# Second attention of a two-layer macaron block: ScalarE passes of one and of two heads, four turns over three PSUM banks, D products issued twice

## The reference, cut to what matters

```
q, k, v = split_heads(x @ Wq.T), split_heads(x @ Wk.T), split_heads(x @ Wv.T)
diff_sq = maximum(|q|^2 + |k|^2 - 2 q.k, 0)
denom   = maximum((1 - |q|^2) * (1 - |k|^2), 1e-6)
cosh    = maximum(1 + 2 * diff_sq / denom, 1)
distance = arccosh(cosh)
attn = softmax(-distance)
out  = merge_heads(attn @ v) @ Wo.T
x = x + out
```

## Time and profile before

| | us |
|---|---|
| median of 3 runs | 3502.58 (3499.26 to 3506.87) |
| the profiled execution | 3507.83 |
| its span, first to last instruction | 3506.1 |
| mean granted TensorE clock over the span | 0.847 |
| busy in the span: PE, DVE, ACT, POOL | 2925.6, 2228.4, 1880.1, 872.3 |
| `relu` (line 1475), first and last start | 1841.0, 3011.5 |

### The profile page before, as it was taken

How to read it: one execution, slowest core, us unless ns; L and a number is a source line. 1 busy time by engine, 2 the same in 40 slices (tenths; PEclk the granted TensorE clock), 3 DMA queues, 4 the chain that set the end, 5 groups by cost and what they waited for, 6 DMA issues and landing times. The chain is left out here.

```text
span 3506.1 us, 52449 instructions
## 1 busy us (share of the span) xinstructions
PE 2925.6 (83%) x17862; PEld 2166.3 (62%) x17862; DVE 2228.4 (64%) x5046; ACT 1880.1 (54%) x1988; POOL 872.3 (25%) x584
## 2 busy tenths in 40 slices
PE   5999968888689996999966878678687777579999
PEld 4888846666578885999963333233333333269998
DVE  5555557777655556666657767676675676366665
ACT  2222246767422222343327888878888788633333
POOL 1000010000000001000015564664655565410000
PEclk9999979999899997999986656666766666689999
DMA  2000000000000001000000000000000000010000
GB/s 79 0 0 0 0 1 1 0 0 0 0 1 0 0 0 48 0 0 0 0 0 1 0 0 0 0 0 0 0 0 0 0 0 0 4 45 0 0 0 24
DMA packets 3188, 17.98 MB, mean 5 GB/s; under 512 B 1088, under 2 KB 2112, under 8 KB 2112
## 3 DMA queue, kind: packets, MB, share of 16 engines
q1 hardware_dynamic: 3136, 17.32, 1.3%
HBM read 15.22 MB, written 2.10 MB: 5 GB/s over the span
## 5 line engine op out<-in xcount | busy, mean ns | idle before, releaser
L1402 POOL TENSOR_TENSOR A_Y<-A_Y,A_U 128x2048 f32<-128x2048 f32 x96 | 433.6, 4548 | 402.0 <-ACT A_U L1444 402.0
L1475 DVE TENSOR_SCALAR A_U<-ps 128x1024 f32<-128x1024 f32 x256 | 309.4, 1219 | 165.2 <-PE ps L1606 83.8
L1618 PE MATMUL ps<-A_QT,A_KT 9*128 9x512 f32 x512 | 275.3, 631 | 127.6 <-DVE A_U L1483 127.2
L140 POOL TENSOR_TENSOR rstd<-var_eps,half_neg 128x4 f32<-128x4 f32 x45 | 49.8, 1106 | 1288.6 <-DVE var_eps L120 1182.4
L1483 DVE SCALAR_TENSOR_TENSOR A_U<-ps,A_U 128x1024 f32<-128x1024 f32 x256 | 311.8, 1218 | 40.4 <-PE ps L1618 40.3
L1606 PE MATMUL ps<-A_QT,A_KT 28*128 28x512 f32 x512 | 249.3, 612 | 100.8 <-DVE A_U L1475 99.4
L257 ACT ACTIVATE F1b_act<-ps 128x512 f32<-128x512 f32 x256 | 153.3, 599 | 247.3 <-PE ps L223 231.2
L257 ACT ACTIVATE F1a_act<-ps 128x512 f32<-128x512 f32 x256 | 153.3, 599 | 242.9 <-PE ps L223 226.6
L1618 PEld LDWEIGHTS ps<-A_QT,A_KT 9*128 9x128 f32 x512 | 112.3, 271 | 251.6 <-DVE A_U L1483 215.4
L1590 PE MATMUL ps<-A_Y,A_VA 128*32 128x512 f32 x768 | 246.0, 779 | 16.7 <-ACT A_Y L1451 16.7
L257 ACT ACTIVATE F0b_act<-ps 128x512 f32<-128x512 f32 x160 | 95.7, 598 | 273.3 <-PE ps L223 273.3
(11 more groups left out here) (338 smaller groups left out, 6634.1 us busy)
## 6 DMA issues: line engine op xcount, KB each, us to landing
dn<-in_down SPq DMA_DIRECT2D x2, 2048.0 KB, 12.1
stage<-in_up SPq DMA_DIRECT2D x1, 2560.0 KB, 9.4
X<-in_x SPq DMA_DIRECT2D x1, 2048.0 KB, 7.7
F1a_up<-in_up SPq DMA_DIRECT2D x1, 2048.0 KB, 8.1
F1b_up<-in_up SPq DMA_DIRECT2D x1, 2048.0 KB, 7.2
out_x<-X SPq DMA_DIRECT2D x1, 2048.0 KB, 6.3
dn<-in_down SPq DMA_DIRECT2D x1, 1280.0 KB, 12.3
qkv_w_s<-in_w_qkv SPq DMA_DIRECT2D x2, 192.0 KB
```

Of the source, the lines that this page charges most:

```text
L1402: eng.tensor_tensor(flat(y_slot(h)), flat(y_slot(h)), flat(Um[:, h % UR]), ALU.add).then_inc(s["t_ready"], 1)
L1475: eng.tensor_scalar(u_half(h, half), d_pair(n), 0.0, None, ALU.max).then_inc(s["dp_vector"], 1)
L1618: last = eng.matmul(ps[:, 4 + b, :], KT[r:r + 9, h // 2, kt * P:(kt + 1) * P], QT[r:r + 9, h // 2, :], start=True, stop=True)
```

## The change

- ScalarE: of each four heads, the first two have square-root passes of their own (2048 elements), the last two a joined one. Ln and Exp stay joined.
- GpSimd: `apply_norm_gpsimd` stands behind the adds of heads 4 to 7 and `assemble_gpsimd`; `keep_norm_gpsimd` behind all adds.
- TensorE: `difference` issues its two products twice, in the order 0, 1, 0, 1, into the same two banks with the same data. `turn_four` does the four turns in front of bursts 0 and 3 over banks 6, 4, 5 and 6, and the pair's outputs follow them in one run. q, k and v are projected into banks 6, 4 and 5 one behind the other, then come all outputs of pair 7, and then the waits for all three takes. In a burst, a pair's outputs are k tile 0 in step 5, k tile 1 in step 6, k tiles 2 and 3 in step 7.
- The back turns of the chunk before start one step earlier in burst 1, and the transposes and scores of its norm move from burst 2 to steps 4 and 5 of burst 3. VectorE's side follows, and its copies of the outputs move into step 4 of bursts 0, 2 and 3.
- New waits: banks 4 and 5 must be free of factor products (`u_ready`), bank 6 of the scores (`lg_copied`) and of the output projection (`x_added`).

The core of the diff:

```
...
-def take_v_vector(eng, k):
+def take_v_vector(eng, k, bank):
     eng.wait_ge(s["v_done"], k + 1)
     eng.wait_ge(s["pvh_done"], k * PAIRS + 1)
...
-        rows_of_bank(ROWS)).then_inc(s["v_taken"], 1)
+        rows_of_bank(bank)).then_inc(s["v_taken"], 1)
...
     eng.wait_ge(s["qk_tr"], k * TURNS + i + 1)
+WINDOW_BANKS = (6, 4, 5, 6)
...
             for h in range(0, 4):
-            if not first:
-                apply_norm_gpsimd(eng, c, last_chunk(c))
             for h in range(4, 8):
-            for h in range(8, 12):
+            if not first:
+                apply_norm_gpsimd(eng, c, last_chunk(c))
+            for h in range(8, H):
             if not first:
-            for h in range(12, H):
-                add(c, h)
+                eng.drain()
...
         def main(c, first):
-            for heads in ((0, 2), (4, 6), (8, 10), (12, 14)):
-                for h in heads:
-                    y, u = y_two(h), u_two(h)
+            for h0 in range(0, H, 4):
+                for h in (h0, h0 + 1, h0 + 2):
+                    joined = h == h0 + 2
+                    y = y_two(h) if joined else flat(y_slot(h))
+                    u = u_two(h) if joined else flat(Um[:, h % UR])
                     if h >= YR:
                         eng.wait_ge(s["pvh_done"], c * PAIRS + (h - YR) // 2 + 2)
                         eng.wait_ge(s["pvh_done"], c * PAIRS + h // 2)
-                    eng.wait_ge(s["u_ready"], c * HALVES + 2 * h + 4)
+                    eng.wait_ge(s["u_ready"], c * HALVES + 2 * h + (4 if joined else 2))
-                    eng.activation(u, u, ACT.Sqrt).then_inc(s["s_ready"], 2)
+                    eng.activation(u, u, ACT.Sqrt).then_inc(s["s_ready"], 2 if joined else 1)
-                for h in heads:
+                for h in (h0, h0 + 2):
                     eng.wait_ge(s["t_ready"], c * H + h + 2 + UR)
...
                     after(i)
-            for i in range(EARLY, EARLY + 4):
-                turned_vector(eng, c, i)
-            if tail:
-                out_copy_vector(eng, c - 1, 2)
+            for i in range(4):
+                turned_vector(eng, c, EARLY + i, WINDOW_BANKS[i])
             def after0(i):
                 if i < 4:
                     turned_vector(eng, c, EARLY + 4 + i)
+                if tail and i == 4:
+                    out_copy_vector(eng, c - 1, 2)
             burst(0, after0)
-            take_q_vector(eng, c + 1, ROWS)
-            take_k_vector(eng, c + 1, ROWS)
+            take_q_vector(eng, c + 1, 6)
+            take_k_vector(eng, c + 1, 4)
+            take_v_vector(eng, c, 5)
             if tail:
-            take_v_vector(eng, c)
             def after1(i):
-                if tail and 1 <= i < 1 + TPC:
-                    divide_vector(eng, c, i - 1)
-                if tail and i == 6:
+                if tail and i < TPC:
+                    divide_vector(eng, c, i)
+                if tail and i == 4:
             burst(1, after1)
...
             if tail:
-            out_copy_vector(eng, c, 0)
             def after2(i):
-                if tail and i == 3:
-                    copy_norm_vector(eng, c)
-                if tail and i == 5:
-                    norm_logits_vector(eng, s, c, before_c, nxt, ROWS)
+                if i == 4:
+                    out_copy_vector(eng, c, 0)
             burst(2, after2)
-            for i in range(0, 4):
-                turned_vector(eng, c + 1, i)
-            out_copy_vector(eng, c, 1)
+            for i in range(4):
+                turned_vector(eng, c + 1, i, WINDOW_BANKS[i])
             def after3(i):
                 if i < 4:
                     turned_vector(eng, c + 1, 4 + i)
+                if i == 4:
+                    out_copy_vector(eng, c, 1)
+                    if tail:
+                        copy_norm_vector(eng, c)
+                if tail and i == 5:
+                    norm_logits_vector(eng, s, c, before_c, nxt, ROWS)
             burst(3, after3)
...
                 if not (first and n < 2):
                     eng.wait_ge(s["dp_vector"], c * HALVES + n - 1)
-                for b in range(2):
+                for b in (0, 1, 0, 1):
...
                 eng.wait_ge(s["turned"], k * TURNS + i)
                 turn_tensor(eng, k, i)
+            def turn_four(k, i0):
+                for i in range(3):
+                    turn_tensor(eng, k, i0 + i, WINDOW_BANKS[i])
+                eng.wait_ge(s["turned"], k * TURNS + i0 + 1)
+                turn_tensor(eng, k, i0 + 3, WINDOW_BANKS[3])
+            def pair_in_burst(n, pair, i):
+                if i in (5, 6):
+                    outputs(n, pair, (i - 5,))
+                if i == 7:
+                    outputs(n, pair, (2, 3))
             ahead(0)
-            turn(c, EARLY)
-            turn(c, EARLY + 1)
-            turn(c, EARLY + 2)
+            eng.wait_ge(s["turned"], c * TURNS + EARLY)
             if not first:
-                outputs(c - 1, 5, (0, 1))
-            turn(c, EARLY + 3)
+                eng.wait_ge(s["lg_copied"], c + 1)
+                eng.wait_ge(s["u_ready"], c * HALVES)
+            turn_four(c, EARLY)
             if not first:
-                outputs(c - 1, 5, (2, 3))
+                outputs(c - 1, 5, (0, 1, 2, 3))
+            eng.wait_ge(s["turned"], c * TURNS + EARLY + 4)
             def after0(i):
                 if i < 4:
                     turn(c, EARLY + 4 + i)
-                if not first and i in (5, 6):
-                    outputs(c - 1, 6, (2 * i - 10, 2 * i - 9))
+                if not first:
+                    pair_in_burst(c - 1, 6, i)
             burst(0, after0)
             ahead(1)
             eng.wait_ge(s["turned"], (c + 1) * TURNS)
             eng.wait_ge(s["xa_ready"], c + 2)
-            project_rows_tensor(eng, xa, 0, ROWS, "q_done")
+            project_rows_tensor(eng, xa, 0, 6, "q_done")
+            eng.wait_ge(s["u_ready"], c * HALVES + 8)
+            project_rows_tensor(eng, xa, 1, 4, "k_done")
+            eng.wait_ge(s["xv_ready"], c + 1)
+            project_rows_tensor(eng, xT_c, 2, 5, "v_done")
             if not first:
-                outputs(c - 1, 7, (0, 1))
+                outputs(c - 1, 7, (0, 1, 2, 3))
             eng.wait_ge(s["q_taken"], c + 2)
-            project_rows_tensor(eng, xa, 1, ROWS, "k_done")
-            if not first:
-                outputs(c - 1, 7, (2, 3))
             eng.wait_ge(s["k_taken"], c + 2)
-            eng.wait_ge(s["xv_ready"], c + 1)
-            project_rows_tensor(eng, xT_c, 2, ROWS, "v_done")
+            eng.wait_ge(s["v_taken"], c + 1)
             def after1(i):
-                if i in (5, 6):
-                    outputs(c, 0, (2 * i - 10, 2 * i - 9))
+                pair_in_burst(c, 0, i)
                 if first:
-                if i == 1:
-                    eng.wait_ge(s["v_taken"], c + 1)
-                if 1 <= i < 1 + TPC:
-                    turn_out_tensor(eng, c, i - 1)
-                if i == 6:
+                if i < TPC:
+                    turn_out_tensor(eng, c, i)
+                if i == 4:
                     turn_back_tensor(eng, c)
             burst(1, after1)
...
             if not first:
                 project_out_tensor(eng, c)
             outputs(c, 1, (0, 1, 2, 3))
-            def after2(i):
-                if i in (5, 6):
-                    outputs(c, 2, (2 * i - 10, 2 * i - 9))
-                if first:
-                    return
-                if i == 3:
-                    turn_norm_tensor(eng, c)
-                if i == 5:
-                    score_tensor(eng, c)
-            burst(2, after2)
+            burst(2, lambda i: pair_in_burst(c, 2, i))
             ahead(3)
             eng.wait_ge(s["asm_done"], c + 2)
-            if first:
-                eng.wait_ge(s["v_taken"], 1)
-            else:
-                eng.wait_ge(s["lg_copied"], c + 2)
-            turn(c + 1, 0)
-            turn(c + 1, 1)
-            turn(c + 1, 2)
-            outputs(c, 3, (0, 1))
-            turn(c + 1, 3)
-            outputs(c, 3, (2, 3))
+            if not first:
+                eng.wait_ge(s["x_added"], c)
+            eng.wait_ge(s["u_ready"], c * HALVES + 24)
+            turn_four(c + 1, 0)
+            outputs(c, 3, (0, 1, 2, 3))
+            eng.wait_ge(s["turned"], (c + 1) * TURNS + 4)
             def after3(i):
                 if i < 4:
                     turn(c + 1, 4 + i)
-                if i in (5, 6):
-                    outputs(c, 4, (2 * i - 10, 2 * i - 9))
+                if not first and i == 4:
+                    eng.wait_ge(s["turned"], (c + 1) * TURNS + EARLY)
+                    turn_norm_tensor(eng, c)
+                if not first and i == 5:
+                    score_tensor(eng, c)
+                pair_in_burst(c, 4, i)
             burst(3, after3)
...
         for pair in range(5, PAIRS):
             outputs(B - 1, pair, (0, 1, 2, 3))
```

(1 more changed line is left out.)

## The result

The changed kernel takes 3537.53 us in the median of five runs (3527.53 to 3540.82), the kernel before 3502.58 beside it; the ratio is 1.009, with a 95% interval from 1.007 to 1.011. I had forecast 3484, faster. The profiled execution took 3537.68, its span is 3535.7 and its mean granted clock 0.832, against 3506.1 and 0.847.

What follows compares the result with a forecast made beforehand. The round was taken as a chain between engines: the hole before burst 2, TensorE-VectorE and TensorE's clock. Bursts 93.3 plus windows 54.5 gave 147.8 us, 2.6 less; over 7.5 rounds, 3502.6 - 19 = 3484, range 3400 to 3570.

Steps and rivals of the forecast that it cites:

- My sum: One main-loop round of the second attention, four bursts 93.3 plus four windows 54.5: 147.8 us, 2.6 less than before.
- Window 0 with burst 0: Stretch up to burst 0's first `relu`, then to its last factor product: window 12.7 us, burst 23.0.
- window 2 with burst 2: Stretch up to burst 2's first `relu`, then to its last factor product: window 11.3 us (was 15.3), burst 20.6.
- window 3 with burst 3: Stretch up to burst 3's first `relu`, then to its last factor product: window 12.7 us, burst 25.6 (was 23.4).
- The hole: VectorE's 8.65 us idle before burst 2, behind GpSimd's norm waiting for `var_eps`; moving the norm was to remove it.
- Window 1: From burst 0's last factor product to burst 1's first `relu`, with q, k, v projections: 17.8 us (was 13.4).
- bursts 1 and 2: First `relu` to last factor product: 24.1 us in burst 1 (was 23.8), 20.6 in burst 2 (was 24.0).
- Tails: End of each burst, from factor 5 to factor 7: 7.3 us cold where it was 9.5.
- The second issue: Doubled D products on TensorE: 0.86 us more cold, 0.45 to 0.6 warm, 32 times a round; worth nothing to the clock.
- the outputs' chain: Window 2's first factor waits behind outputs 1: 8.3 + 4.5 + 0.8, less 2.3 for two `relu`, 11.3 us.
- The clock: TensorE's granted clock in windows, taken as before: 0.99, 0.86, 0.72, 0.87; all cold gives 3638 us, all warm 3350.
- rival B: Split outputs no longer lift TensorE's clock; 1.2 GHz in half the windows, 9.5 us more a round, 3554; chance 0.26.

Runs made afterwards that it cites:

- e14: The changed kernel with the addition of EPS (`var_eps`) taken from VectorE and given to GpSimd, in front of its power; 3473.7 us.
- e9: The changed kernel, D still issued twice, with a pair's outputs in a burst as two k tiles in step 6 and two in step 7; 3430.6 us.
- e3: The changed kernel, D still issued twice, with a pair's outputs as two k tiles in step 5 and two in step 6, as before; 3398.3 us.
- e8: The changed kernel with ScalarE's square-root passes joined for both pairs, as before the change; mean round 153.62 us.
- e13: The kernel before with only ScalarE's mixed passes of the change; slower by 3.4 us a round, 153.60 us.
- e4: The changed kernel with D issued once and a pair's outputs as two k tiles in step 5 and two in step 6; 3354.47 us.
- e12: e4 with a square-root pass of its own for every head; 3348.96 us.
- e6: e4 with ScalarE's square-root passes joined for both pairs, as in the kernel before; mean round 139.95 us.
- e10: e3 with the first of the two D issues over all 128 rows, overwritten by the second; mean round 139.95 us, 5 us longer than e3.
- e5: The changed kernel with the first of the two D issues over all 128 rows, overwritten by the second; 3492.8 us.

## Why the prediction was wrong

My sum was 147.8 us a round; 153.6 came. In pairs of a window and its burst, forecast and measured: 0: 35.7 and 34.0; 1: 41.9 and 41.7; 2: 31.9 and 37.5; 3: 38.3 and 40.4.

Window 0 with burst 0 was 1.7 us too dear in the sum; window 2 with burst 2 was 5.6 and window 3 with burst 3 was 2.1 too cheap.

**What held.** GpSimd's first add starts 3.8 us after the group's first pass (I said 3.7), the joined pair is ready at 14.3 (14.6) and the last add ends at 23.5 (23.7), by the changed kernel's timeline from 2158.61. The hole is gone. Window 1 is 17.2 (17.8), bursts 1 and 2 are 24.5 and 20.9 (24.1 and 20.6). Tails are 7.5 (7.3). The second issue gives the clock nothing over the whole, as I let it.

**The step that failed** is window 2, in the sum 11.3; 16.6 came. The sum let the outputs' chain end last there: D and projection, then outputs 1 and the first factor. The other chain, D and projection, then "add back and statistics 2.4", came to 8.3 + 2.4 = 10.7 and was taken as covered. In the changed kernel this other chain ends last: 4.7 us to the first D, 3.7 for D, 2.1 for the projection, and 6.1 from the projection's end to `relu`. 2.4 us was the cost of these instructions with VectorE left alone. The same move that I credited with the 8.65 us hole puts GpSimd's adds beside `var_eps`, which then takes 3.77 us; that is 3.6 of the difference. D and projection at 1.2 GHz, where I took 2.4 and 1.5, are 1.9 more, and the way to the first D 0.3. The outputs' chain with its measured pieces (4.7, 3.7, 2.0, 5.2 and 0.7, less 2.3) would have come to 14.0.

e14, which takes `var_eps` off VectorE, comes to 145.0 us a round and 3473.7 us, near my forecast for the change, 3484. That is luck in part: its round is 2.7 us under my sum, and its clock is not that of the changed kernel either.

The Trainium skill, "SBUF — State Buffer", section "Who interferes with whom", says that VectorE and GpSimd share a pair of ports that one of them locks for a whole instruction, that `tensor_scalar` from SBUF to SBUF can need the pair, and that the one who comes second blocks until it is free. The trace agrees: 3.77 us, ending 0.03 after the add. By that rule `relu` and `scale`, which read PSUM, are left alone, and so they are: their means are 1218 and 1216 ns where the kernel before has 1219 and 1218.

**The clock** was the second error. I took windows 2 and 3 near the clock that before's windows had the earlier trace rows. Window 3 and burst 3 together are 2.1 us over the sum, and D at 3.8 instead of 2.4 with turns at 3.6 instead of 3.1 makes 1.9 of that. Window 3 by itself is the 12.7 of the sum: its `relu` starts early, VectorE then waits 2.1 us for the first factor, and the loss shows in burst 3, 27.7 where I had 25.6.

```profile
2236.53 3.78 PE L1611 MATMUL ps<-A_QT,A_KT 28*128 28x512 f32 x8
2240.23 1.11 PE L1316 MATMUL ps<-ident,up_hi 128*128 128x128 f32 x4
...
2243.84 4.48 PE L1595 MATMUL ps<-A_Y,A_VA 128*32 128x512 f32 x16
```

These are TensorE's D products, the first of its turns and the outputs behind them in window 3 of the changed kernel. This is rival B's mechanism, in two windows of four, and e9 shows its place: the split of the outputs. But the square above says that the split does so only together with `var_eps` on VectorE; with `var_eps` on GpSimd the same split has 0.80 and 0.79. So B as I had written it, a loss by the split alone, is not what happens.

**What stays open** is how the hold and the clock are tied. In chunk 1 of the two profiles, the changed kernel and e14 have the same lengths up to window 2 within 0.04 us a stretch (10.2, 24.7, 17.4, 24.5), and TensorE issues the same work. Yet 2.4 GHz comes 3.8 us into window 2 in e14, and 13.9 into it in the changed kernel. The hold starts 12.9 us into this window, so it cannot be what kept the clock down before that. The other way round is possible: with the outputs, D and projection as fast as in e14, `var_eps` would have come 3.0 us earlier (9.9 us into the window and not 12.9; an estimate from the two timelines), at 2204.2 in the round shown above, where GpSimd was idle from 2203.6 to 2206.4. A warm window 2 would then not have been held at all. No run tests that by itself. The D products of this window, in order of time, first of the changed kernel, then of e14:

```profile
2045.24 3.78 PE L1611 MATMUL ps<-A_QT,A_KT 28*128 28x512 f32 x8
```

```profile
2044.51 2.10 PE L1614 MATMUL ps<-A_QT,A_KT 28*128 28x512 f32 x8
```

My reading is that window 2 stands at an edge where a shift of a few tenths decides; it is not shown. That all rounds of the changed kernel fall on the cold side and those of e14 on the other, is seen in one trace of each, and the times of five runs each (3527 to 3541 and 3459 to 3485) agree with it; why, no run here shows.

## What to carry to other kernels

When a wait of GpSimd is removed, look at which small VectorE instructions from SBUF to SBUF now run beside its long ones; one of them in front of a burst cost up to 4.26 us here (e3), nearly a whole GpSimd add. Don't add its price to that of a slow clock in the same window: the two can hide each other. Where the clock goes to and fro, try to keep long runs of full-row products in one piece at the end of a burst (e9 against the change: 13.7 us a round), and ask of each window what lifts its clock before pricing it with the old one. And find the floor of the other engines first: it tells which parts of a change can pay only once another part is gone.

## What was not expected of the hardware

- A busy TensorE is not a warm one: 914 us of 1000 at a granted clock of 0.63 (changed), 767 at 0.67 (before). With the first D issue over 128 rows instead of 28 it is 0.72, busy for 927.
- A four-element VectorE instruction took 0.17 us alone and 3.77 beside a GpSimd add of 4.55.
- Mean round lengths fall on few values. The changed kernel, e8 and e13 have 153.62, 153.62 and 153.60 us, e4 and e12 129.72 and 129.71, e6, e9 and e10 139.95 each, e5 and the later rounds of e14 146.77 and 146.75, though they do different work. In e6, e8 and e10 only the mean does so, single rounds differ by up to 5.4 us. In such a loop a small edit can be swallowed whole or cost several us at once, and I would not trust a term of 1 us a round; what sets these lengths no run here tests.
